# The split and transpose of x1: from TensorE, ScalarE and VectorE to one DMA transpose per tile

## The reference

```
h1 = causal attention, 16 heads of 16, over x, with one image key and value per sequence, then a projection
a1 = layernorm(linear attention(h1) + h1) * gamma + beta
x1 = x + a1
h2 = LSTM over the 64 steps of x1, started from cond (256 units, gates from x1 @ Wx and h @ Wh)
out = x1 + FFN(h2)        # fp4 quantised, silu(gate) * up, then down
```

## Time and profile before

| | us |
|---|---|
| median of 3 runs (1059.33 to 1062.59) | 1059.73 |
| the profiled execution's own time | 1062.53 |
| its span, first to last instruction | 1060.5 |
| DVE busy | 920.3 (87%) |
| PE busy | 895.4 (84%) |
| ACT busy | 506.7 (48%) |
| POOL busy | 344.2 (32%) |
| DMA queue 1, share of 16 engines | 9.9% |

### The profile page before, as it was taken

One profiled execution on the slowest core, in us unless ns is written; L12 is line 12 of the kernel. 1 busy time (PEld: TensorE's weight loads), 2 busy tenths in 40 slices (PEclk: granted clock), 3 DMA queues, 4 the chain that ended last, 5 costly groups with the idle time before them and its releaser, 6 DMA issues.

```text
span 1060.5 us, 27568 instructions
## 1 busy us (share of the span) xinstructions
PE 895.4 (84%) x9862; PEld 599.7 (57%) x9862; DVE 920.3 (87%) x2157; ACT 506.7 (48%) x1177; POOL 344.2 (32%) x436
## 2 busy tenths in 40 slices
PE   3477887988988888888987899999999999999974
PEld 1254654766666666666654555565565556555542
DVE  5489889899999999999984689888888988888883
ACT  2256446466666666667653334434333343433321
POOL 0135456355555555555542011110111111111111
PEclk9589679799999999999998999999999999999987
DMA  4501000010111001110110000000000000000000
GB/s 104 190 13 29 19 19 29 23 33 18 32 32 32 28 21 32 32 32 21 30 31 16 1 11 21 21 21 20 20 16 15 21 20 21 20 20 19 15 19 25
DMA packets 37143, 30.37 MB, mean 29 GB/s; under 512 B 12081, under 2 KB 35953, under 8 KB 37076
## 3 DMA queue, kind: packets, MB, share of 16 engines
q1 hardware_dynamic: 37076, 29.42, 9.9%
HBM read 20.87 MB, written 8.54 MB: 28 GB/s over the span
## 4 chain that ended last, share of the span: by engine, by line
PE 22%; DVE 15%; issue 8%; ACT 4%; POOL 1%; DVEq 0%; POOLq 0%; ACTq 0%
PE bank L987 6%; PE bank L711 5%; PE bank L886 4%; PE bank L875 4%; DVE fc L1461 4%; DVE hqT L1523 2%; DVE h_value L171 2%; ACT hqT L1182 2%; DVE ig L1463 2%; DVE x_value L171 1%; DVE cell L1465 1%; ACT h L1157 1%; POOL ffn_room L663 1%; PE bank L979 1%; PE bank L866 1%
## 5 line engine op out<-in xcount | busy, mean ns | idle before, releaser
L663 POOL TENSOR_TENSOR ffn_room<-h_value,h_scale 128x704 f32<-128x704 f32 x32 | 45.7, 1428 | 382.0 <-DVE h_value L171 382.0
L711 PE MATMUL bank<-gu,xqT 128*128 128x512 f16 (+1 forms) x576 | 130.1, 366 | 0.0
L886 PE MATMUL bank<-wh,h 128*64 128x512 f16 x768 | 95.1, 383 | 1.9 <-ACT h L1157 1.9
L875 PE MATMUL bank<-wx,x1T 128*64 128x512 f16 x768 | 93.8, 379 | 0.9 <-DVE x1T L440 0.9
L611 POOL TENSOR_TENSOR p<-prob,p 128x520 f16<-128x520 f32 x64 | 78.7, 1230 | 43.2 <-ACT p L1065 43.2
L1147 ACT ACTIVATE sig<-bank 128x256 f32<-128x256 f32 x64 | 24.6, 384 | 139.5 <-PE bank L886 138.9
L987 PE MATMUL bank<-dn,hqT 128*128 128x256 f16 x576 | 71.5, 280 | 22.5 <-DVE hqT L1523 22.5
L875 PEld LDWEIGHTS bank<-wx,x1T 128*64 128x64 f16 x768 | 78.5, 201 | 11.6 <-DVE x1T L440 1.2
L711 PEld LDWEIGHTS bank<-gu,xqT 128*128 128x128 f16 x576 | 54.4, 99 | 52.8 <-issue 11.3
L1461 DVE TENSOR_TENSOR fc<-sig,cell 128x128 f32<-128x128 f32 x64 | 52.4, 818 | 34.4 <-ACT sig L1147 34.4
L776 PE MATMUL bank<-ident,p 128*65 128x128 f16 x1024 | 78.8, 228 | 1.5 <-POOL p L611 0.8
(11 more groups left out here) (201 smaller groups left out, 2220.9 us busy)
## 6 DMA issues: line engine op xcount, KB each, us to landing
x_in<-in_x SPq DMA_DIRECT2D x32, 128.0 KB, 2.2
x_res<-in_x SPq DMA_DIRECT2D x32, 128.0 KB, 2.1
x_rows<-x_rows_sb SPq DMA_DIRECT2D x32, 128.0 KB, 1.9
ffn_room<-x_rows SPq DMA_DIRECT2D x64, 64.0 KB, 2.2
out<-ffn_room SPq DMA_DIRECT2D x64, 64.0 KB, 2.0
mask_in<-in_mask_Bx1x1xS_ff SPq DMA_DIRECT2D x64, 16.0 KB, 2.4
x1T<-in_L_cond_Wx SPq DMA_DIRECT2D x1, 1024.0 KB, 6.5
x1T<-in_L_cond_Wh SPq DMA_DIRECT2D x1, 1024.0 KB, 8.5
```

The lines of the kernel that those rows point to most:

```text
L663: pool.tensor_tensor(blocks(hq, FF), blocks(fp4_h.value, FF), spread(fp4_h.scale, FF), ALU.mult).then_inc(s["hq_ready"], 1)
L711: last = pe.matmul(dst, lhs(a, c), rhs(b, c), start=first and c == 0 and a == b, stop=c == C - 1 and (a, b) == parts3[-1], skip_group_chec ...
L875: last = pe.matmul(bank[e][B * h:B * h + B, :], x1T16[m][:, c, :, at], half_cols(wx16, a, c, h), start=False, stop=True, skip_group_check= ...
L886: last = pe.matmul(bank[e][B * h:B * h + B, :], h16[:, m, c, :], half_cols(wh16, a, c, h), start=False, stop=True, skip_group_check=True)
```

## The change

The two fp16 parts of x1 are made in row layout, before the transpose. ACT copies x1_rows to fp16 (x1_split part 0), POOL subtracts it from x1_rows to give part 1, and SP issues one DMA transpose of both parts, 128 rows by 512 fp16 values, straight into the array that the LSTM reads. PE's transpose, ACT's and DVE's reads of bank 2 and the waits on them go. `x1_split` is one buffer: ACT waits for the transpose of the tile before. The store of x1_rows stays as it is.

```diff
-    x1T16 = [sb(f"x1T16_{i}", [P, C, B, S], F16) for i in range(2)]
+    x1T_all = sb("x1T16", [P, 2, C, B, S], F16)
+    x1T16 = [x1T_all[:, i] for i in range(2)]
+    x1_split = sb("x1_split", [P, 2, D], F16)
-    def x1_part(eng, t, part):      # and its calls at the end of ACT's and DVE's steps
...
 SP, in step, after x_res
             if t5:
                 sp.wait_ge(s["x1_ready"], t5.count())
                 sp.dma_start(x1_tiles[t5.number()], x1_rows[:, :]).then_inc(s["x1_stored"], 16)
+                sp.wait_ge(s["x1_lo"], t5.count())
+                sp.dma_start_transpose(x1T_all[:, :, :, bass.ds(t5.number() * 2, 2), :].rearrange("p i c b s -> p (i c) (b s)"),
+                                       x1_split[:, :, :].rearrange("p i d -> p (i d)")).then_inc(s["x1T_in"], 16)
...
 POOL, in step
-                after(pool, s["x1_ps"], t5.count(back=1))
...
                 pool.tensor_tensor(rstd[:, :], var_eps[:, :], neg_half[:, :], ALU.pow).then_inc(s["rstd_ready"], 1)
+            if t5:
+                pool.wait_ge(s["x1_hi"], t5.count())
+                pool.tensor_tensor(x1_split[:, 1, :], x1_rows[:, :], x1_split[:, 0, :], ALU.subtract).then_inc(s["x1_lo"], 1)
             if t1:
                 shift(t1, 0)
...
 PE
-            after(pe, s["x1T_lo"], t.count(back=5))             # in qkv
-                if not t1:
-                    pe.wait_ge(s["x1T_lo"], t5.count(back=1))
-                rows_transpose(t5, bank[2][:, D:2 * D], x1_rows, "x1_ready", "x1_ps")
-        pe.wait_ge(s["x1T_lo"], NT)
+        pe.wait_ge(s["x1T_in"], 16 * NT)
...
 ACT, in step, after exp(t2, 0) and probs_hi(t2, 0)
+            if t5:
+                act.wait_ge(s["x1_ready"], t5.count())
+                after(act, s["x1T_in"], t5.count(per=16, nth=16, back=1))
+                act.copy(x1_split[:, 0, :], x1_rows[:, :]).then_inc(s["x1_hi"], 1)
```

More of the change, by code:

```diff
@@ L225, in program @@
     eps_ln = sb("eps_ln", [P, 1])
-    x1T16 = [sb(f"x1T16_{i}", [P, C, B, S], F16) for i in range(2)]
-    x1T_room = [t[:, :, :, :].rearrange("p c b s -> p (c b s)").bitcast(F32) for t in x1T16]
+    x1T_all = sb("x1T16", [P, 2, C, B, S], F16)
+    x1T16 = [x1T_all[:, i] for i in range(2)]
+    x1T_room = [t.rearrange("p c b s -> p (c b s)").bitcast(F32) for t in x1T16]
     bias_cols = sb("bias_cols", [P, BIAS_C])
@@ L324, in program @@
         kv_ps kv_masked ctx_ps den_ready den_inv ctx_div resid stats_ready mean_ready var_ready
-        rstd_ready z_ready zg_ready xb_ready x1_ready x1_ps x1T_hi x1T_lo x1_stored
+        rstd_ready z_ready zg_ready xb_ready x1_ready x1_hi x1_lo x1T_in x1_stored
         gates_ps sig_if sig_o tanh_g i_g cell_ready tanh_c h_ready h_hi h_lo
@@ L431, in program @@
     parts3 = ((0, 0), (0, 1), (1, 0))
-    def x1_part(eng, t, part):
[L435 to L441, removed]
     def mask_count(t):
@@ L1134, in step @@
                     ffn_hi(t5, "end")
-                act.wait_ge(s["x1_ps"], t5.count())
-                x1_part(act, t5, 0)
         pipeline(act, 5, step, first=10)
@@ L1449, in step @@
                     ffn_lo(t5, "end")
-                dve.wait_ge(s["x1T_hi"], t5.count())
-                x1_part(dve, t5, 1)
             chore(t1, 1)
```

## The result

| | before | after |
|---|---|---|
| median of the runs | 1059.5 us (4 runs, 1058.1 to 1062.6) | 1195.9 us (4 runs, 1194.4 to 1197.0) |
| ratio, 95% interval | 1 | 1.1276 (1.1254 to 1.1298) |
| span of the profiled execution | 1060.5 us | 1193.2 us |
| steady step of the first part (tiles 10 to 31, 21 steps) | 14.83 us | 20.46 us |
| second part (from the LSTM's first product) | 482.6 us | 482.95 us |

The forecast was 1240 us with a range of 1150 to 1325.

A forecast was written before the change was run, and what follows sets the result against it. DVE was taken to bound the steady steps before; SP's new wait closes a loop. 23 x (4.1 + 2.7) = 156, 4 x 4.1 = 16, end 8 - 1 = 7: +180 on 1060.5 gives 1240 us, range 1150 to 1325.

The forecast's parts named there:

- The clock: PE after its wait for x_in: linear_kv and part of q/k/v at 1.2 GHz, 2.7 us more per step.
- The ring share: x_in's load goes through the same DMA engines behind the transpose's 128 KB: 0.6 us more, bounds 0 to 4.3.
- Rival 2: Slow transpose keeps the DMA engines 3 us longer, x_in lands behind it: 81 us more, 1320 us; chance 0.18.
- The transpose's issue: SP's queue, from issue of the transpose to issue of x_in: 1.0 us, taken near the pair of masks (1.17).
- 4 steps to tiles 5 to 8 (chores): Steps where DVE's weight work hides a slow q/k/v: only the longer loop counts, 4 x 4.1 = 16 us.
- 23 steps to tiles 9 to 31: Steps with both the longer loop and the slow clock: 23 x (4.1 + 2.7) = 156 us more.
- tile 31 to the LSTM, and the second part: End of the first part: 5 us later, 3 us of slow clock in the LSTM, drain steps give back 1: 7.
- a clock that holds: PE keeps full clock despite its gaps, leaving only the longer loop: 1176 us; chance 0.13.
- The faster case: SP's wait is free and DVE's saved 0.33 us a step counts: 1050 us; chance 0.04.
- The point that it named, 313.3: Time on POOL before which x1_lo must be done so that x_in is there at 316.7 and SP's wait is free.
- ACT's copy: ACT's new 128x256 copy, about 0.37 us, covered by idle gaps of 0.57 and 0.36 us ahead of exp and q/k copy.
- the signs: Expected in the profile: steps of 20 to 23 us, PE idling some 4 us for x_in, clock well under 1.00.

The follow-up runs named there:

- e4: Kernel before plus one SP wait for rstd_ready ahead of the store of x1_rows, without split or DMA transpose: 1158.6 us, ratio 1.0958.
- e1: Changed kernel, but SP issues each tile's transpose one step later, behind the next tile's loads: 1071.9 us, ratio 1.0139.
- e2: Changed kernel, but POOL makes x1's low part right after xb_rows, ahead of rstd, with SP's order kept: 1052.0 us, ratio 0.9952.
- e3: Changed kernel with linear_q done five times in steps 4 to 30 to fill PE's idle time: 1149.6 us, ratio 1.0876.
- e9: Changed kernel with a plain DMA copy for the transpose (transposition left out) and linear_q done five times: 1139.9 us, ratio 1.0769.
- e5: Changed kernel with the DMA transpose replaced by a plain DMA of the same bytes, transposition left out: 1192.4 us, ratio 1.1250.
- e7: Changed kernel with POOL's low part right after xb_rows, and ACT's high part of x1 moved behind v's: 1045.6 us, ratio 0.9880.
- e8: Changed kernel with linear_q done three times to fill part of PE's idle time: 1186.5 us, ratio 1.1208.

## Why the prediction was right, and where it was 44 us off

The cause was right: x_in is issued behind x1's low part, this stands behind rstd, and each late x_in delays the next mean_var. e4 shows that a wait at that place suffices, e1 and e2 that the stall for x_in is gone without it (e1 keeps 1.4%, of another kind), e3 that the clock adds to it. These terms of one step, measured from 405.45 to 426.09, stand against the forecast's:

| term of the loop | forecast | measured |
|---|---|---|
| x_in at PE to the split of q/k, slow clock included | 5.1 + 2.7 = 7.8 | 6.85 |
| split of q/k to the end of mean_var | 8.34 | 8.25 |
| to the end of x1's low part | 1.62 | 1.54 |
| to SP's issue of the transpose | 0.17 | 0.14 |
| issue of the transpose to issue of x_in | 1.0 | 1.79 (1.41 in every other step, mean 1.57) |
| issue of x_in to PE | 2.2 + 0.6 = 2.8 | 2.07 |
| step | 21.7 | 20.64 (mean 20.46) |

Three terms were mis-sized.
- *The clock*, 2.7: e3 gives 1.92. The end of the slow stretch, "within q/k/v", was right; linear_kv (2.77 us) is slow throughout, and from 409.80 us on the clock is 1.00.
- *The ring share*, 0.6: the transpose does not hold x_in up at all (2.0 us to landing). Rival 2 is out by the same row.
- *The transpose's issue*, 1.0: too small by 0.4 to 0.8, 0.57 in the mean. I took the pair of masks as the nearest row; one transpose keeps SP's queue for 1.21 us and a little behind that. Of this, 0.5 is dearer than a plain copy of the same bytes (1.57 against 1.07).

The rule that I cited, that transposing DMAs are as fast as regular ones (the Trainium skill, Advanced Engine Details and Errata, X-Bar Transpose), holds for the time to landing, 2.4 us in both kernels; of the issue it says nothing, and there e9 shows the difference. Its worth was estimated at 12 us; e9 gives 9.7 with the clock held, e5 3.5 without, inside its interval.

By stretch, the extra time of the two profiled executions:

| stretch, by x_in's transposition | forecast | measured |
|---|---|---|
| start to tile 4 | 0 | 0.4 |
| 4 steps to tiles 5 to 8 (chores) | 16 | 6.7 |
| 23 steps to tiles 9 to 31 | 156 | 120.1 |
| tile 31 to the LSTM, and the second part | 7 | 5.1 + 0.35 |
| sum | 180 | 132.7 |

Of the 36 us missing in the 23 steps, 21 x (6.8 - 5.63) = 25 are the terms above. Another 10 are one step that I had counted like the rest, from tile 8 to 9. In the kernel before it takes 24.38 us, in the changed one 21.19; the busy time of this step, before and then after:

```profile
172.94:197.32 24.38, 18.36 (x210) 13.23 (x209) 21.12 (x42) 9.99 (x22) 13.93 (x14) 0.68 0.06 19
```

```profile
180.03:201.22 21.19, 15.22 (x206) 9.90 (x207) 16.91 (x39) 9.78 (x21) 11.54 (x13) 0.82 0.10 28
```

Before had slow clock and idle time of its own here, and could not lose the same again. The same holds for the chore steps (4.1 each forecast, 1.7 measured): the forecast took the steady step as their starting point without reading their own intervals in the trace of before. No experiment separates what in them hides the stall.

The rivals: a clock that holds (1176 forecast) is what e3 builds, at 1149.6. The faster case (1050) turned on x1's low part being done early enough, and it comes true in e2 (1052.0) and e7 (1045.6) as soon as POOL does that. The point that it named, 313.3, is not tested: in e2 the low part is ready 6.1 us before PE's transposition of x_in. The working of the point is also 0.5 us too generous, as it lets x_in land at 316.7 where PE begins its transposition at 316.16; with 316.16 the point is 312.8.

Two lesser statements did not hold. ACT's copy was said to be covered by the gaps in front of it. In the stalled loop nothing shows against that, but at full pace it is wrong: e7 is 0.22 us a step faster than e2 by moving that copy alone. And among the signs, SP was to wait for x1's low part and not for xb_rows; it waits for both, and the second is off the loop.

## What to carry to other kernels

Ahead of a wait in the queue that issues loads, ask which load stands behind it and whether what is waited for depends, over any engine, on the load before: if it does, the step becomes the length of that loop, and no engine's busy time shows it. Take each changed stretch's own time before as its base, not that of the steady steps. A piece of work cut out of a stalled loop must be tried with TensorE's clock held as well: the same saving gives 3.5 us in e5, within the noise, and 9.7 in e9.

## What the runs showed of the hardware beyond this

- **The clock falls after shorter idle times than the trace of before had shown, and sometimes late.** There the shortest was 3.22 us. Here it falls in every steady step of e4, around waits for x_in of 2.4 to 3.4 us, and in e8 in 19 of the 22 steps of tiles 10 to 31, after 2.6 to 3.1 us, in the one shown 1.4 us after the work had resumed. In the other three, after 2.64 to 2.72 us, it holds, so the length of the wait alone does not decide there. It holds in all steady steps of e3, after 1.2 to 1.8 us. The Trainium skill (TensorE: Matmul & The Clock Gate, HAM oscillation) describes the loop in which each DMA wait sets the clock back; the granted clock of 0.83 over the steady steps agrees, and e5 adds that a shorter wait need not shorten the slow stretch behind x_in.
- **DVE's busy time depends on what POOL does beside it.** Over 21 steady steps DVE is busy 273.6 us in the changed kernel and 300.7 in e2, with the same 777 operations. Two operations make most of these 27.1 us: by their mean times, 18.2 and 8.1 us in 21 steps. DVE groups by line (count | busy us, mean ns | idle before), the changed kernel and then e2:

```profile
L1440 DVE TENSOR_SCALAR z_rows<-res_rows,mean_var,rstd 128x256 f32<-128x256 f32 x21 | 15.7, 750 | 0.0
...
L1360 DVE TENSOR_TENSOR o_rows<-o_sum,o_rec 128x128 f32<-128x128 f32 x21 | 6.1, 292 | 0.0
```

```profile
L1440 DVE TENSOR_SCALAR z_rows<-res_rows,mean_var,rstd 128x256 f32<-128x256 f32 x22 | 25.0, 1136 | 0.0
...
L1360 DVE TENSOR_TENSOR o_rows<-o_sum,o_rec 128x128 f32<-128x128 f32 x21 | 24.3, 1157 | 0.0
```

  In one step of e2 the second runs from 412.15 to 413.31 us, beside POOL's 128x520 shift (412.11 to 413.17); in the changed kernel the shift is over before the operation begins. The Trainium skill (SBUF — State Buffer, Who interferes with whom) says that a DVE operation with two inputs in SBUF contends with a GpSimd operation that reads SBUF: o_rows agrees, 0.29 us alone and 1.16 beside the shift. The first operation, z_rows, is no case of an idle POOL: it runs beside a POOL operation in both kernels and ends 0.14 to 0.15 us behind it, behind the 0.67 us of x_split at 422.09 in the changed kernel (422.23), behind the 1.06 us of the shift at 410.29 in e2 (410.44).

  That some 18 us of DVE's busy time in the steady steps of e2 are this waiting was not in the prediction, and no run was made to move it. e1 moves it in passing: there o_rows of 128x128 takes 0.28 us, but each of the pair behind it 0.93 instead of 0.70, DVE is busy 281.7 us, and the step is no shorter (15.14).
